# Maxima of self-attention carried for each half of the queries, and eight hidden units of the choice of tokens computed among its gates

## The chip, the cores and the metric

The kernel runs on one core of a Trainium2 chip, as one program. The metric is the time of a run on the device in microseconds (us); the median of three runs is given. A profiled execution gives the trace.

## The reference

Two decoder layers on x of 4 x 1024 tokens with 256 features. Each layer has self-attention, cross-attention and a feed-forward part with experts, each added to its input and followed by a layer norm. What the change touches:

```python
# layer 0, self-attention: 16 heads of 16 features, rotated q and k, causal
scores = jnp.einsum('bhqd,bhkd->bhqk', q, k) * scale
scores = jnp.where(causal, jnp.finfo(scores.dtype).min, scores)
out = jnp.einsum('bhqk,bhkd->bhqd', jax.nn.softmax(scores, axis=-1), v)

# layer 1, differential self-attention: 16 heads, two sets of q and k of 8 features, no mask
a = attend(q1, k1) - lam * attend(q2, k2)
a = a * rsqrt(mean(a * a) + eps) * rms_weight * (1.0 - LAMBDA_INIT)

# layer 1, expert choice: each expert takes 512 of the 1024 tokens of a batch
gate_scores = jax.nn.softmax(x @ w_gate_w + w_gate_b, axis=-1)
...
route = masked / denom * capacity
_, seq_ids = jax.lax.top_k(route_eb, K)
h = jax.nn.gelu(einsum('ebkd,edh->ebkh', xg, W1) + b1, approximate=False)
o = einsum('ebkh,ehd->ebkd', h, W2) + b2
```

## The kernel before

x stays in SBUF as X, 128 partitions by 32 tiles of tokens by 256 features. The stages run one after the other: self-attention (`attention`: `project`, `attend`, `merge`), cross-attention, experts, twice. In the second layer the experts are `expert_choice`: `choose` and `take`.

**`attend`.** It works on groups of four score rows s (four heads of a batch, or in the second layer two heads with two sets each): 16 groups in the first layer and 32 in the second. Queries come in two halves q of 512, keys in tiles of 128. A group has NS slots: 12 in the causal layer (four for q = 0, eight for q = 1, the diagonal ones with 512, 384, 256 and 128 columns) and 16 in the other. In a slot TensorE makes the four scores of one key tile and one half of the queries (line 739), in one of four banks psS each, and ScalarE turns each into exponentials (line 612); one or two slots later TensorE multiplies them by V (line 760), for which GpSimd cuts the diagonal blocks first (line 573). At the end of a half ScalarE copies the sum (line 633), TensorE turns it back (line 778), ScalarE copies that (line 628), VectorE inverts the sums (line 706) and GpSimd scales, squares and adds up.

The exponentials need the maximum of each query's scores. That is subtracted inside the score product: rows TOP and TOP + 1 of the operand Q hold the maxima in two parts, with rows of ones in K. So for each group the scores are also made with queries on the partitions (line 789, four products a slot, in two double banks psM), and VectorE reduces them, two reductions a slot (line 695, or line 689 where a block is masked), into `tops`. When all 2 x NS pairs of a group are done, `combine` (line 700) makes `negm`, 32 columns; TensorE turns it (line 798, 32 x 128), ScalarE copies it twice (line 620, rounded, and line 621), GpSimd subtracts one from the other (line 564), and the SyncE queue writes the rows into Q with eight DMAs (line 510).

What sets the order is written by hand: every engine walks the same turns. In turn t stand the maxima of group t in all slots, the scores of group t - 1 from slot LATE = 5 on, and those of group t - 2 before that. `turn_maxima`, `cut` and the rows of group t - 1 stand in slot 0 of turn t. Banks of psS go round in the order in which their contents are freed, and the list `taken` fixes it. The loads of the group after the next (lines 157 and 158, 16 DMAs) stand in the SyncE queue before the rows.

**`choose`.** X is turned in eight pieces (line 2565), ScalarE copies each to XT (line 2620), and TensorE makes the gates' logits (line 2574, 16 products of 8 columns a piece) for two halves h of the tiles. VectorE's chain makes routes of each half; ScalarE gives its exponentials (line 2625). Routes are turned (line 2592), and a search of 16 steps on VectorE, with a small product of TensorE in each (line 2610), finds the threshold of each expert; then VectorE makes the selection (line 2745). The hidden layer for all tokens is computed in 32 units (line 2585), with an activation Gelu on ScalarE each (line 2639): five units between the two turned routes, one in each step of the search, the rest after it. `take` starts with line 2785.

## Time and profile before

| | us |
|---|---|
| runs | 3478.0, 3486.63, 3487.77 |
| median | 3486.63 |
| the profiled execution, its time | 3496.01 |
| its span from the first instruction to the last | 3493.9 |
| first self-attention, `attend` | 132.9 to 624 |
| second self-attention, `attend` | 1275 to 2546 |
| `choose` | 3286.9 to 3401.5 |

Times in the trace are us from the start of the span. PE is TensorE, PEld its weight load, DVE VectorE, ACT ScalarE, POOL GpSimd, SPq the DMA queue of SyncE. A row of a timeline has the start, the duration with the tail of the last instruction, and the idle time before with what ended it; where instructions overlap, their durations do so too. The granted clock is 1.00 at 2.4 GHz and 0.50 at 1.2 GHz.

### The profile page before, as it was taken

To read this page: it belongs to the slowest core of one execution; us is meant where nothing else is said; L and a number is where in the kernel's file an instruction comes from. 1 tells how busy PE (TensorE), PEld (TensorE's weight loads), DVE (VectorE), ACT (ScalarE), POOL (GpSimd) and SP (SyncE) were. 2 spreads that over 40 slices of the span, in tenths; PEclk is the share of its full clock that TensorE was granted. 3 is DMA by queue.
4 is the path that set the end of the run, shared out by engine and by line. 5 is a ranking of instruction groups with operands and counts; after the bars stand their busy time and mean duration, and the time that the engine had idled before them with its cause. 6 is when DMAs were issued, how large, how long until landed. Compare 5 with 4: busy or idle time off the path is not lost. (4 is left out here: it accounts for less than half of the span.)

```text
span 3493.9 us, 63847 instructions
## 1 busy us (share of the span) xinstructions
PE 3160.6 (90%) x23976; PEld 1627.6 (47%) x23976; DVE 2756.2 (79%) x4703; ACT 2099.0 (60%) x4192; POOL 960.8 (27%) x1622
## 2 busy tenths in 40 slices
PE   7599999678499879999999999999968699999699
PEld 4244444444288533333333333333347454544546
DVE  7788886447677798999999999999557677776466
ACT  3178888245333226999999999999937233334130
POOL 4234433124333430111111111111132334445000
PEclk9699999878699977999999999999989899999789
DMA  4422220000000240010010010000003401000001
GB/s 167 137 53 65 65 59 21 28 1 1 25 1 1 94 140 20 21 29 20 21 30 20 20 29 21 20 26 24 2 20 121 149 26 51 26 26 1 17 1 48
DMA packets 69412, 143.97 MB, mean 41 GB/s; under 512 B 20752, under 2 KB 33872, under 8 KB 68976
## 3 DMA queue, kind: packets, MB, share of 16 engines
q1 hardware_dynamic: 64752, 135.70, 13.0%
q8 instruction: 189, 3.10, 0.4%
q10 hardware_dynamic: 4352, 4.20, 0.4%
q14 instruction: 119, 0.97, 0.1%
HBM read 83.07 MB, written 54.53 MB: 39 GB/s over the span
## 5 line engine op out<-in xcount | busy, mean ns | idle before, releaser
L612 ACT ACTIVATE L_parts<-L_attn_psS 128x512 f32<-128x512 f32 (+3 forms) x2816 | 1409.5, 573 | 146.5 <-PE L_attn_psS L739 104.2
L695 DVE TENSOR_REDUCE L_attn_tops<-L_attn_psM 128x2 f32<-128x1024 f32 x1152 | 1325.9, 1214 | 60.5 <-PE L_attn_psM L789 57.5
L789 PE MATMUL L_attn_psM<-L_K,L_Q 30*128 30x512 f32 (+4 forms) x2816 | 866.5, 492 | 63.7 <-PEq L199 27.2
L739 PE MATMUL L_attn_psS<-L_Q,L_K 32*128 32x512 f32 (+4 forms) x2816 | 876.3, 474 | 2.2 <-ACT L_parts L612 0.9
L760 PE MATMUL L_attn_psS<-L_parts,L_attn_V 128*32 128x256 f32 (+1 forms) x10752 | 855.6, 390 | 5.4 <-ACT L_parts L612 0.6
L739 PEld LDWEIGHTS L_attn_psS<-L_Q,L_K 32*128 32x128 f32 (+1 forms) x2816 | 408.4, 185 | 556.4 <-ACT L_parts L612 270.1
L789 PEld LDWEIGHTS L_attn_psM<-L_K,L_Q 30*128 30x128 f32 (+1 forms) x2816 | 389.2, 190 | 110.4 <-DVE L_attn_tops L695 58.7
L760 PEld LDWEIGHTS L_attn_psS<-L_parts,L_attn_V 128*32 128x32 f32 x10752 | 214.6, 108 | 354.6 <-issue 186.8
L689 DVE CUSTOM_DVE_ANT_0 L_attn_psM<-L_attn_psM,L_attn_wide 128x384 f32<-128x384 f32 (+3 forms) x512 | 236.5, 522 | 19.0 <-PE L_attn_psM L789 18.5
L2276 ACT ACTIVATE x_E<-x_psS 128x512 f32<-128x512 f32 x256 | 138.9, 595 | 184.3 <-PE x_psS L2399 170.7
L2322 DVE TENSOR_REDUCE x_tops<-x_psM 128x2 f32<-128x1024 f32 x128 | 153.2, 1206 | 92.5 <-PE x_psM L2428 92.4
L2238 POOL TENSOR_TENSOR x_acc<-x_acc,x_E 128x512 f32<-128x512 f32 x128 | 171.9, 1343 | 182.4 <-ACT x_E L2276 180.2
L1539 PE MATMUL m_psE<-m_wp,m_xp 128*128 128x512 f32 x768 | 182.1, 394 | 2.8 <-DVE m_z L1673 2.8
L573 POOL TENSOR_SCALAR_AFFINE_SELECT L_parts<-L_parts 128x128 f32<-128x128 f32 x512 | 146.4, 294 | 125.6 <-ACT L_parts L612 119.0
L564 POOL TENSOR_TENSOR L_attn_mparts<-L_attn_mT,L_attn_mparts 32x128 fp32r<-32x128 f32 x48 | 21.5, 449 | 567.3 <-ACT L_attn_mT L621 567.3
L544 POOL TENSOR_TENSOR L_attn_recs<-L_attn_rec,L_attn_sign 128x16 f32<-128x16 f32 x64 | 14.3, 223 | 575.1 <-DVE L_attn_rec L706 575.1
L2395 PE MATMUL x_psS<-x_Q,x_K 64*128 64x512 f32 x864 | 150.5, 438 | 11.4 <-ACT x_E L2276 11.4
L1539 PEld LDWEIGHTS m_psE<-m_wp,m_xp 128*128 128x128 f32 x768 | 142.6, 189 | 34.6 <-DVE m_z L1673 5.7
L2448 PE MATMUL x_psO<-x_E,L1x_VL 128*64 128x512 f32 x512 | 145.3, 647 | 0.0
L2395 PEld LDWEIGHTS x_psS<-x_Q,x_K 64*128 64x128 f32 x864 | 75.0, 190 | 144.8 <-ACT x_E L2276 94.5
L2428 PE MATMUL x_psM<-x_K,x_Q 64*128 64x512 f32 x768 | 118.2, 406 | 23.3 <-DMA x_K<-L1x_kTc 20.4
L324 PE MATMUL L_proj_psQ<-L_AO,L_proj_wqk 128*128 128x512 f32 x256 | 125.0, 614 | 15.4 <-DMA L_AO<-in_L_sin 12.2
(363 smaller groups left out, 4131.7 us busy)
## 6 DMA issues: line engine op xcount, KB each, us to landing
parts_q<-L_parts SPq DMA_DIRECT2D x64, 256.0 KB
parts_k<-L_parts SPq DMA_DIRECT2D x64, 256.0 KB
L_Q<-parts_q SPq DMA_DIRECT2D x192, 64.0 KB
L_K<-parts_k SPq DMA_DIRECT2D x192, 64.0 KB
L_Q<-parts_q SPq DMA_DIRECT2D x64, 128.0 KB
L_K<-parts_k SPq DMA_DIRECT2D x64, 128.0 KB
queries<-x1p_qo SPq DMA_DIRECT2D x16, 512.0 KB, 3.5
keys<-x1p_ko SPq DMA_DIRECT2D x16, 512.0 KB, 4.4
```

Source lines behind the costliest of these rows:

```text
L573: pool.affine_select(block, block, [[1, P]], ALU.is_ge, 0.0, base=0, channel_multiplier=-1).then_inc(e_cut, 1)
L612: act.activation(E[(4 * n + s) % (4 * RING)][:, c0:], psS[bank][:, c0:], ACT.Exp, scale=scale).then_inc(e_done, 1)
L689: last = dve.tensor_tensor_reduce(part, part, wide[:, HALF - n:], 1.0, LOWEST, ALU.add, ALU.max, tops[:, row, h:h + 1])
L695: dve.tensor_reduce(dst, src, AX, ALU.max).then_inc(m_read, 1)
L739: pe.matmul(psS[bank][:, c0:], K[g.slot][r:r + RH, c, kt * P:(kt + 1) * P], Q[g.slot][r:r + RH, c, q * HALF + c0:(q + 1) * HALF], start=Tr ...
L760: last = pe.matmul(psS[bank_of["O", at, q]][32 * s:32 * s + 32, lo:hi], V[g.slot][:, kt, s // shared, :], E[(4 * n + s) % (4 * RING)][:, l ...
L789: last = pe.matmul(psM[bank][:, j * HALF:j * HALF + n], Q[t.slot][r:r + TOP, c, qt * P:(qt + 1) * P], K[t.slot][r:r + TOP, c, h * HALF:h * ...
L1539: last = pe.matmul(psE[e][:], xp[u.slot][:, i, c, k * P:(k + 1) * P], wp[:, j, c, e * HALF:(e + 1) * HALF], start=(n + c == 0), stop=(n == ...
L2238: pool.tensor_tensor(to[:], to[:], e[:], ALU.add).then_inc(sums[1], 1)
L2322: dve.tensor_reduce(dst[:, :, t, h], src, AX, ALU.max).then_inc(m_read, 1)
L2395: pe.matmul(banks[h][:], K[k][rows, x, kt * P:(kt + 1) * P], Q[k][rows, y, cols], start=(j == 0), stop=False, skip_group_check=True)
L2448: last = pe.matmul(psO[LD * h:LD * h + LD, :], v, tile(s, h)[:], start=(kt == 0), stop=(kt == TB), skip_group_check=True)
```

## The change

In `attend` the pairs of the maxima are put in order of the halves: all those of q = 0 first. Each half has its own combine (line 703 after the change, a maximum of two halves of `tops`, 16 columns, no negation; the blank rows of K become -1 in place of 1), its own transpose of 16 x 128, one copy by ScalarE, a rounding copy and a subtraction on GpSimd, and its own row DMAs: four in the first layer and two in the second. The combine stands between the two reductions of a slot: slots 4 and 12 after the group's first in the first layer, 8 and 16 in the second. The scores of a group begin LAG = 12 slots after its first maxima, in both layers (17 and 21 before); those of its second half four and eight slots later. The turns give way to one loop over slots. The loads of the next group but one stand between the rows of a group's second half and those of the next one's first.

In `choose` eight of the 32 hidden units stand in the loop of the gates, one after each piece, in the two halves of psR; their activations stand between the copies of XT and around the exponentials.

```diff
-                    pool.memset(K[k][:].bitcast(F32), 1.0).then_inc(blank, 1)
+                    pool.memset(K[k][:].bitcast(F32), -1.0).then_inc(blank, 1)
...
+    of_half = [sum(t // 4 == q for _, t, _, _, _ in pairs) for q in range(2)]
...
-    LATE = 5
+    LATE = 4
+    LAG = max(of_half[0] // 2 + LATE, NS + LATE - (ends[0] + 1))
...
+        B_AT = [LAG + BACK + ends[0] + 3 - BACK, LAG + BACK + ends[1] + 2]
+        SLOTS = groups * NS + B_AT[1] - NS + 4
...
+        T_AT = [of_half[0] // 2, NS]
+        SUM_AT = LAG + BACK
...
+                def cut(g, q):
+                    pt, done = mparts[q][g % 2], 2 * (2 * g + q)
+                    pool.wait_ge(e_done, freed["T", g, q])
...
+                    pool.tensor_copy(pt[:, 0, :], mT[q][g % 2][:]).then_inc(m_cut, 1)
+                    pool.wait_ge(m_cut, done + 1)
+                    pool.tensor_tensor(pt[:, 1, :], mT[q][g % 2][:], pt[:, 0, :].bitcast(F32), ALU.subtract).then_inc(m_cut, 1)
...
-                    act.activation(mparts[k][:, 0, :], psS[bank][0:4 * TB, 0:P], ACT.Copy).then_inc(m_cut, 1)
-                    act.activation(mT[k][:], psS[bank][0:4 * TB, 0:P], ACT.Copy).then_inc(e_done, 1)
+                    act.activation(mT[q][g % 2][:], psS[bank][0:16, 0:P], ACT.Copy).then_inc(e_done, 1)
...
-                    dve.tensor_reduce(negm[t.slot][:], tops[:], AX, ALU.max, negate=True).then_inc(m_neg, 1)
+                    dve.tensor_tensor(most_of[q][g % 2][:], tops[:, q, :, :, 0], tops[:, q, :, :, 1], ALU.max).then_inc(m_most, 1)
...
-                    pe.transpose(psS[bank][0:4 * TB, 0:P], negm[g % 3][:], ident[:]).then_inc(s_done, 1)
+                    pe.transpose(psS[bank][0:16, 0:P], most_of[q][g % 2][:].rearrange("p s t -> p (s t)"), ident[:]).then_inc(s_done, 1)
...
+        EARLY = NB
+        hidden_bank = lambda n: psR[:, n % 2 * HALF:(n % 2 + 1) * HALF] if n < EARLY else psH[n % 4]
...
                     gates(n)
+                    hidden(n)
                 turned_routes(0)
-                todo = iter(range(UNITS))
+                todo = iter(range(EARLY, UNITS))
...
-                for n in range(6):
-                    copied(n)
-                exponents(0)
-                for n in range(6, NB):
-                    copied(n)
+                copied(0)
+                for n in range(EARLY):
+                    if n + 1 < NB:
+                        copied(n + 1)
+                    if n == 4:
+                        exponents(0)
+                    rectified(n)
                 exponents(1)
```

On VectorE in the second self-attention, the kernel before: reductions of maxima, the combine of a group and the two inversions.

```order
L695 TENSOR_REDUCE L_attn_tops<-L_attn_psM 128x2 x16
L706 RECIPROCAL L_attn_rec<-L_attn_ob 128x16
L695 TENSOR_REDUCE L_attn_tops<-L_attn_psM 128x2 x12
L700 TENSOR_REDUCE L_attn_negm<-L_attn_tops 128x32
L695 TENSOR_REDUCE L_attn_tops<-L_attn_psM 128x2 x4
L706 RECIPROCAL L_attn_rec<-L_attn_ob 128x16
L695 TENSOR_REDUCE L_attn_tops<-L_attn_psM 128x2 x16
```

The same place after the change:

```order
L703 TENSOR_TENSOR L_attn_most<-L_attn_tops 128x16
L690 TENSOR_REDUCE L_attn_tops<-L_attn_psM 128x2
L696 RECIPROCAL L_attn_rec<-L_attn_ob 128x16
L690 TENSOR_REDUCE L_attn_tops<-L_attn_psM 128x2 x15
L703 TENSOR_TENSOR L_attn_most<-L_attn_tops 128x16
L690 TENSOR_REDUCE L_attn_tops<-L_attn_psM 128x2
L696 RECIPROCAL L_attn_rec<-L_attn_ob 128x16
```

The one combine of a group has become two of half the width, each one reduction ahead of the end of its slot.

On TensorE at the transpose of the maxima in the second self-attention, before (psS holds scores and sums, psM the maxima's products):

```order
L739 MATMUL L_attn_psS<-L_Q,L_K 128x512
L789 MATMUL L_attn_psM<-L_K,L_Q 128x512
L760 MATMUL L_attn_psS<-L_parts,L_attn_V 32x256 x4
L798 MATMUL L_attn_psS<-ident,L_attn_negm 32x128
L739 MATMUL L_attn_psS<-L_Q,L_K 128x512
L789 MATMUL L_attn_psM<-L_K,L_Q 128x512
```

And after:

```order
L732 MATMUL L_attn_psS<-L_Q,L_K 128x512
L774 MATMUL L_attn_psM<-L_K,L_Q 128x512
L752 MATMUL L_attn_psS<-L_parts,L_attn_V 32x256 x4
L783 MATMUL L_attn_psS<-ident,L_attn_most 16x128
L732 MATMUL L_attn_psS<-L_Q,L_K 128x512
L774 MATMUL L_attn_psM<-L_K,L_Q 128x512
```

The transpose stands at the end of a slot as before, with 16 rows in place of 32, and comes twice a group in place of once (every 82 rows in place of 163).

On TensorE in the gates loop of `choose`, before, its last rounds and what follows (each unit of the hidden layer is two products here):

```order
L2565 MATMUL f_psT<-ident,X 128x128 x8
L2574 MATMUL f_psG<-f_wg,f_XT 128x8 x8
L2565 MATMUL f_psT<-ident,X 128x128 x8
L2574 MATMUL f_psG<-f_wg,f_XT 128x8 x16
L2592 MATMUL f_psR<-ident,f_routes 128x128 x4
L2585 MATMUL f_psT<-f_XT,f_w 128x512 x10
L2592 MATMUL f_psR<-ident,f_routes 128x128 x4
```

And after:

```order
L2559 MATMUL f_psG<-f_wg,f_XT 128x8 x8
L2572 MATMUL f_psR<-f_XT,f_w 128x512 x2
L2550 MATMUL f_psT<-ident,X 128x128 x8
L2559 MATMUL f_psG<-f_wg,f_XT 128x8 x8
L2572 MATMUL f_psR<-f_XT,f_w 128x512 x2
L2559 MATMUL f_psG<-f_wg,f_XT 128x8 x8
L2572 MATMUL f_psR<-f_XT,f_w 128x512 x2
L2580 MATMUL f_psR<-ident,f_routes 128x128 x4
L2572 MATMUL f_psT<-f_XT,f_w 128x512 x10
L2580 MATMUL f_psR<-ident,f_routes 128x128 x4
```

Each round has got a hidden unit, in psR; the five units between the turned routes have stayed, and the tail after the search has eight products in place of 24.

On ScalarE in the same loop, before:

```order
L2620 ACTIVATE f_XT<-f_psT 128x2x512 x6
L2625 ACT_TABLE_LOAD
L2625 ACTIVATE f_ex<-f_less 128x4x32
L2620 ACTIVATE f_XT<-f_psT 128x2x512 x2
L2625 ACTIVATE f_ex<-f_less 128x4x32
L2635 ACTIVATE L1f_B<-f_b 32x1024
L2636 ACTIVATE f_b2h<-f_b 32x1024
L2639 ACT_TABLE_LOAD
L2639 ACTIVATE L1f_HT<-f_psT,f_b 128x512 x32
```

And after, from the fourth activation on:

```order
L2616 ACTIVATE L1f_HT<-f_psR,f_b 128x512
L2609 ACTIVATE f_XT<-f_psT 128x2x512
L2621 ACT_TABLE_LOAD
L2621 ACTIVATE f_ex<-f_less 128x4x32
L2616 ACT_TABLE_LOAD
L2616 ACTIVATE L1f_HT<-f_psR,f_b 128x512
L2609 ACTIVATE f_XT<-f_psT 128x2x512
L2616 ACTIVATE L1f_HT<-f_psR,f_b 128x512
L2609 ACTIVATE f_XT<-f_psT 128x2x512
L2616 ACTIVATE L1f_HT<-f_psR,f_b 128x512 x2
L2621 ACT_TABLE_LOAD
L2621 ACTIVATE f_ex<-f_less 128x4x32
```

The two exponentials stand amid the activations now, with a table load on either side of each.

## Rows read from the trace of the kernel before

**Rows 1.** The page, busy time, share of the span and instructions of each engine
```profile
PE 3160.6 (90%) x23976; PEld 1627.6 (47%) x23976; DVE 2756.2 (79%) x4703; ACT 2099.0 (60%) x4192; POOL 960.8 (27%) x1622
```

**Rows 2.** The page, costliest groups: busy, mean ns of one, idle before, releaser
```profile
L612 ACT ACTIVATE L_parts<-L_attn_psS 128x512 f32<-128x512 f32 (+3 forms) x2816 | 1409.5, 573 | 146.5 <-PE L_attn_psS L739 104.2
L695 DVE TENSOR_REDUCE L_attn_tops<-L_attn_psM 128x2 f32<-128x1024 f32 x1152 | 1325.9, 1214 | 60.5 <-PE L_attn_psM L789 57.5
```

**Rows 3.** Windows: busy us of PE, PEld, DVE, ACT, POOL; granted clock; DMA; GB/s
```profile
1275.00:1360.00 85.00, 69.15 (x325) 22.76 (x325) 73.98 (x70) 25.37 (x47) 3.20 (x10) 0.50 0.10 29
1500.00:1800.00 300.00, 298.76 (x3126) 119.17 (x3127) 294.54 (x278) 284.48 (x558) 49.31 (x144) 1.00 0.09 23
3290.00:3330.00 40.00, 34.82 (x167) 34.82 (x167) 8.45 (x69) 8.77 (x9) 0.00 (x0) 0.50 0.10 29
1036.00:1045.00 9.00, 9.00 (x53) 7.68 (x52) 7.61 (x20) 2.96 (x5) 2.97 (x3) 1.00 0.01 4
```

**Rows 4.** Timeline, VectorE, second self-attention: start, us, instruction, idle before it
```profile
1330.66 1.23 DVE L695 TENSOR_REDUCE L_attn_tops<-L_attn_psM 128x2 f32<-128x1024 f32 x1 [0.51 <-PE L_attn_psM L789]
...
1815.13 0.22 DVE L700 TENSOR_REDUCE L_attn_negm<-L_attn_tops 128x32 f32<-128x64 f32 x1
...
1818.06 2.36 DVE L695 TENSOR_REDUCE L_attn_tops<-L_attn_psM 128x2 f32<-128x1024 f32 x2 [0.24 <-PE L_attn_psM L789]
...
2494.23 0.22 DVE L700 TENSOR_REDUCE L_attn_negm<-L_attn_tops 128x32 f32<-128x64 f32 x1
```

**Rows 5.** Timeline, ScalarE, second self-attention
```profile
1817.34 0.27 ACT L620 ACTIVATE L_attn_mparts<-L_attn_psS 32x128 fp32r<-32x128 f32 x1
1817.52 0.25 ACT L621 ACTIVATE L_attn_mT<-L_attn_psS 32x128 f32<-32x128 f32 x1
...
1819.02 2.09 ACT L612 ACTIVATE L_parts<-L_attn_psS 128x512 f32<-128x512 f32 x4 [0.17 <-PE L_attn_psS L739]
...
1855.07 0.27 ACT L620 ACTIVATE L_attn_mparts<-L_attn_psS 32x128 fp32r<-32x128 f32 x1
...
2545.64 0.60 ACT L628 ACTIVATE L_attn_ob<-L_attn_psS 128x512 f32<-128x512 f32 x1 [0.75 <-PE L_attn_psS L778]
```

**Rows 6.** Timeline, ScalarE, first self-attention
```profile
198.15 0.25 ACT L621 ACTIVATE L_attn_mT<-L_attn_psS 32x128 f32<-32x128 f32 x1
...
225.92 0.25 ACT L621 ACTIVATE L_attn_mT<-L_attn_psS 32x128 f32<-32x128 f32 x1
...
229.63 1.66 ACT L612 ACTIVATE L_parts<-L_attn_psS 128x384 f32<-128x384 f32 x4 [0.30 <-PE L_attn_psS L739]
...
234.80 1.57 ACT L612 ACTIVATE L_parts<-L_attn_psS 128x512 f32<-128x512 f32 x3 [0.72 <-PE L_attn_psS L739]
...
622.57 0.60 ACT L628 ACTIVATE L_attn_ob<-L_attn_psS 128x512 f32<-128x512 f32 x1 [0.75 <-PE L_attn_psS L778]
```

**Rows 7.** Timeline, SyncE's queue and VectorE, first self-attention
```profile
226.72 6.22 SPq L510 DMA_DIRECT2D L_Q<-L_attn_mparts  x8
...
584.55 0.22 DVE L700 TENSOR_REDUCE L_attn_negm<-L_attn_tops 128x32 f32<-128x64 f32 x1
```

**Rows 8.** Timeline, TensorE, choice of tokens
```profile
3295.18 1.97 PE L2565 MATMUL f_psT<-ident,X 128*128 128x128 f32 x8 [6.34 <-DMA L1f_w<-in_L1f_w]
...
3333.71 1.09 PE L2592 MATMUL f_psR<-ident,f_routes 128*128 128x128 f32 x4
...
3379.58 20.85 PE L2585 MATMUL f_psT<-f_XT,f_w 128*128 128x512 f32 x48
3401.46 0.70 PE L2785 MATMUL f1t_psS<-L1f_sel,L1f_onehot 32*128 32x512 f32 x2 [1.03 <-PEq L2538]
```

**Rows 9.** Timeline, ScalarE and VectorE, choice of tokens
```profile
3318.29 1.28 ACT L2625 ACT_TABLE_LOAD   x1
...
3400.47 0.69 ACT L2639 ACTIVATE L1f_HT<-f_psT,f_b 128x512 f32<-128x512 f32 x1 [1.03 <-PE f_psT L2585]
...
3385.84 1.23 DVE L2745 TENSOR_TENSOR L1f_sel<-f_tie,f_gt 128x1024 fp32r<-128x1024 bf16 x1
```

More of the change, by code:

```diff
@@ L429, in attend @@
-        lam_sign = sems.sem(f"{tag}_attn_lam_sign")
-        def run(turn):
-            for g in range(groups + 2):
-                turn(At(g, None, 3), g < groups, 1 <= g <= groups, g >= 2)
+        sem = lambda name: sems.sem(f"{tag}_attn_{name}")
+        v_blank, t_blank = sem("v_blank"), sem("t_blank")
+        maskin, masks = sem("maskin"), sem("masks")
+        mx = [[sem(f"mx{q}{k}") for k in range(2)] for q in range(2)]
+        v_in = sem("v_in")
+        s_done = sem("s_done")
+        e_done, e_cut = sem("e_done"), sem("e_cut")
@@ new lines, in attend, with at @@
+        passed = sem("passed")
+        o_done = sem("o_done")
+        o_rec, o_sign, o_scaled, o_norm = sem("o_rec"), sem("o_sign"), sem("o_scaled"), sem("o_norm")
+        m_done, m_read = sem("m_done"), sem("m_read")
+        m_most, m_cut = sem("m_most"), sem("m_cut")
+        lam, lamin, lam_sign = sem("lam"), sem("lamin"), sem("lam_sign")
+        B_AT = [LAG + BACK + ends[0] + 3 - BACK, LAG + BACK + ends[1] + 2]
+        SLOTS = groups * NS + B_AT[1] - NS + 4
+        def at(slot, offset, length=NS):
+            g, k = divmod(slot - offset, NS)
+            return (g, k) if 0 <= g < groups and k < length else None
@@ L436, in cuts, with event, group @@
+        def event(slot, offset):
+            return slot >= offset and (slot - offset) % NS == 0 and (slot - offset) // NS < groups
+        def group(slot, offset):
+            return (slot - offset) // NS
+        T_AT = [of_half[0] // 2, NS]
+        SUM_AT = LAG + BACK
         def cuts(g, n):
-            return g.times(4 * sum(diagonal), 4 * sum(diagonal[:n]))
-        def in_turn(new, last):
-            return range(NS if new or last else LATE + BACK + 4)
+            return g * 4 * sum(diagonal) + 4 * sum(diagonal[:n])
@@ new lines, in attend @@
+        for slot in range(SLOTS):
+            exp, summed = at(slot, LAG), at(slot, SUM_AT)
+            if exp:
+                left += [exp + (s,) for s in range(4)]
+                taken += [exp + (s,) for s in range(2)]
+            if summed and (summed[1] == 0 or summed[1] - 1 in ends):
+                taken.append(("O", summed[0], steps[summed[1]][0]))
+            if exp:
+                taken += [exp + (s,) for s in range(2, 4)]
+            for q in range(2):
+                if event(slot, T_AT[q]):
+                    taken.append(("T", group(slot, T_AT[q]), q))
+                    left.append(("T", group(slot, T_AT[q]), q))
+            if summed and summed[1] in ends:
+                left.append(("O", summed[0], steps[summed[1]][0]))
+            for q in (1, 0):
+                if event(slot, B_AT[q]):
+                    taken.append(("B", group(slot, B_AT[q]), q))
+                    left.append(("B", group(slot, B_AT[q]), q))
@@ L513, in _, with rows @@
-                run(turn)
-                for k in range(3):
-                    n = len(range(k, groups, 3))
-                    sp.wait_ge(mx[k], 128 * n)
+                def rows(g, q):
+                    sp.wait_ge(m_cut, 2 * (2 * g + q) + 2)
+                    for j in range(2):
+                        for c in range(NQ):
+                            to = Q[g % 3][TOP + j:TOP + j + (HP - 1) * RH + 1:RH, c, q * HALF:(q + 1) * HALF]
+                            src = mparts[q][g % 2][c * 4 * HP:(c + 1) * 4 * HP, j, :]
+                            sp.dma_start(to.bitcast(F32), src.bitcast(F32)).then_inc(mx[q][g % 2], 16)
@@ new lines, in _ @@
+                load_group(sp, keep, dh, 1)
+                for g in range(groups):
+                    if g >= 1:
+                        rows(g - 1, 1)
+                        if g + 1 < groups:
+                            if g == 2:
+                                for k in range(4):
+                                    sp.wait_ge(parts_out[k], 256)
+                            if g >= 2:
+                                sp.wait_ge(s_done, s_at[g - 2, NS - 1, 3] + 1)
+                            load_group(sp, keep, dh, g + 1)
+                    rows(g, 0)
@@ L518, in _ @@
+                rows(groups - 1, 1)
+                for q in range(2):
+                    for k in range(2):
+                        sp.wait_ge(mx[q][k], ROWS * (groups // 2))
             @block.gpsimd
@@ L764, in product @@
                         last.then_inc(o_done, 1)
-                def products(t, n, last, old, half):
-                    j = n - LATE - BACK
-                    if j >= 0 and last:
-                        product(t.base - 1, j, half)
-                    if j < 0 and old:
-                        product(t.base - 2, NS + j, half)
                 def turn_back(g, q):
```

319 lines of the change are left out of this document (126 added, 193 removed).

## The prediction

> **What bounds the kernel now.** I read the page's shares first: TensorE is busy for 90% of the span, VectorE for 79%, ScalarE for 60% [rows 1]. Averages hide the stages, so next come the costliest groups: the exponentials of self-attention (2816 of 0.573 us) and the reductions of its maxima (1152 of 1.214 us, and the reader sees there that 57.5 of their 60.5 us of idle time end with a maxima product of TensorE) [rows 2]. Then the windows. In the steady part of the second self-attention (16 slots a group, 32 groups) 300 us hold 298.76 us of TensorE, 294.54 of VectorE and 284.48 of ScalarE [rows 3]: three engines full at once, so a microsecond taken from one of them alone is worth little, and what counts there is how many slots there are and what fills them. From the copy of one group's maxima to the next takes 1855.07 - 1817.34 = 37.73 us, 2.357 a slot [rows 5]; two reductions take 2.36 with their tail, 2.27 from start to start [rows 4]. The filling stands at a clock of 0.50 (1275 to 1360), where mixed reductions of 1.23 us follow 1.74 us apart, each after 0.51 us for TensorE, that is 3.48 us a slot against 2.357 [rows 3, 4]. Last comes the choice of tokens. There the token searches end with the selection at 3385.84 + 1.23 = 3387.07, but TensorE has 48 hidden products (12 units of four) left at 3379.58, for 20.85 us, and the taking of tokens starts at 3401.46 [rows 8, 9]: TensorE's tail is what is late, by 14.4 us.
>
> **Part 1, a shorter lag in the second layer.** A group's scores may start when its maxima lie in Q's rows. Before, that was 21 slots after its first maximum (16 + 5); by halves it is 12 (8 + 4). So nine slots of maxima alone leave the start and nine of scores alone leave the end, and nine slots in which both run come in. Maxima alone cost the reductions, 2.27. Scores alone: from the last combine at 2494.23 to the last copy back at 2545.64 are 51.4 us for some 22 slots, 2.33 each [rows 4, 5]. 9 x (2.27 + 2.33 - 2.357) = 20.2 us less. Nothing hides these; they are the path itself.
>
> **Part 2, the steady group of the second layer.** VectorE's one combine (0.22) becomes two of half the output, which read 32 values and not 64 a partition; not shown, so between 0.09 each (the smallest step beside it) and 0.22; I take 0.15, no change. ScalarE's two copies (0.27 and 0.25, 0.43 from start to end, and soon after them 0.17 us of waiting for TensorE's late scores) become one copy at each of two places: between 2 x 0.20 and 2 x 0.50 against 0.75 now [rows 5]. TensorE gets a second transpose of some 0.2 us. GpSimd gets a second subtraction and two rounding copies; it is busy for 27% of the span and has time [rows 1]. The new wait is TensorE's: the transpose stands at the end of the slot between whose two reductions the combine was made. Queued behind it are the next slot's scores, and ScalarE waits for these. Before, the combine was 2.0 us old at that place (1815.13 + 0.22 to the copy at 1817.34); now it is only one reduction old, so the transpose may wait up to 0.3. Behind a transpose VectorE had 0.24 us of idle time [rows 4]. Per group -0.35 to +0.25 us, -11 to +8 over 32; between like ends I take zero.
>
> **Part 3, the first layer.** The lag goes from 17 slots to 12. A group takes 226.17 - 198.40 = 27.8 us here (the copies' ends), 2.31 a slot; the end of the stage, from the last combine at 584.55 to 622.57, has 38 us in some 17 slots, 2.2 each, and the start, all reductions, I take at 1.95, since the half-masked ones are short. 5 x (1.95 + 2.2 - 2.31) = 9 us less [rows 6, 7]. Against it stands the wait for the rows. The second half's transpose comes at the end of slot 0, its scores at slot 4: three slots of narrow scores (384, 256 and 128 columns), and those before 234.80, of the same widths, ran from 229.63: 5.2 us, which VectorE's masked reductions may make 6.3. What must fit: the copy, 0.25; GpSimd's two steps, 0.8 (from the copy's end at 226.17 to SP's first row at 226.72, with the one of now between, are 0.55); four row DMAs of 6.22 / 8 = 0.78 each, 3.1; and their landing. Before, the eight were issued until 226.72 + 6.22 = 232.94 and the scores' exponential came at 234.80, so landing is at most 1.9 [rows 6, 7]. Sum 6.1: from nothing to 0.9 us late per group. VectorE's slots of the first half are now all masked ones, at their densest just there, and the second transpose finds ScalarE without work in store (its 0.72 us of idle time at 234.80 says so). I take 0.8 us a group between 0.3 and 1.1, x16 = +13. SP's queue: the 16 loads of the next group stand between the two halves' rows, 12 us at the price of a row, and the first half's rows are due eight slots after their transpose (18 us), so that they hide; if that cover went, each microsecond would be paid 15 times. The first layer gives -9 + 13 = +4 (-4 to +9).
>
> **Part 4, eight hidden units earlier in the choice.** The tail shrinks from 12 units to 4: 8 x 20.85 / 12 = 13.9 us less, and selection and TensorE then end together, 3387 against 3386.5, so the cover is gone exactly: a ninth unit would have brought nothing. The eight units are paid in the gates loop. It ran from 3295.18 to 3333.71, 38.5 us, all of it at a clock of 0.50 though TensorE was 87% busy [rows 3, 8], 5.0 us a round. At full clock, twice as fast, a round is 2.5 plus a unit of 1.74, 4.25 us; eight of these less the first transposes, 0.9, make 33.1. At half clock all along it is 38.5 + 8 x 3.44 = 66. The trace doesn't show which; the nearest row is the experts' stretch 1036 to 1045, where dense products, transposes and gate products alternate at 1.00 [rows 3]. I take one round at half clock: 37.4, or -1.1. On ScalarE the exponentials now stand amid the hidden units' activations, and the table is loaded twice more, 1.28 us each [rows 9]. The first pair is hidden under the loop. The second half's exponential stands behind the last early unit and its activation: 1.74 + 0.69 + 1.28, less some 0.9 that VectorE's subtraction of the maxima needs in that time anyway, +2.8, and VectorE's chain, the search and the selection shift by it. Net -13.9 - 1.1 + 2.8 = -12.2, from -16 to +16.
>
> The Trainium skill speaks against this part. "TensorE: Matmul & The Clock Gate", Part 4, says that a transpose on TensorE doesn't count as busy as other products do, and Part 1 that the gate's default is the throttled one, released by activity. By that rule a loop of which much is transposes keeps the low clock; the 0.50 under 87% agrees with it, the 1.00 at 1036 does so only if the dense products between hold the clock up. By the rule at its strictest this part would give +16 and not -12.2.
>
> **Sum.** -20.2 + 0 + 4 - 12.2 = -28.4 us: 3496.0 to 3467.6 for the profiled execution. That one stood 9.4 above the median of the runs, so 3486.6 - 28.4 = 3458 for a median. GpSimd's squares, which the change's name speaks of, are not in the diff; they bring nothing.
>
> **Rivals.** (a) The gates loop stays at half clock throughout. For it: the 38 us at 0.50. Against: 1036 to 1045. Then part 4 is +27.5 + 2.8 - 13.9 = +16 and the whole -20.2 + 4 + 16 = 0: 3487. (b) Each half's transpose, and its rows, stall TensorE. The mechanism: a transpose that waits for a combine only one reduction old, behind it the scores, behind these ScalarE with at most four banks in store; twice a group, 96 times in all. I priced it at zero and 0.8. If it is 0.6 us a transpose in both layers, 48 x 1.2 = 58 us stand against -20.2 - 9 - 12.2 = -41: +17, 3503. It decides from 41 / 48 = 0.86 us a group. For it: VectorE has only 0.7 us of room in a group of 37.7. Against: scores were hardly waited for before, and at slot 1 ScalarE's idle time was 0.17. (c) The low clock at the start of the second self-attention, 33 us at 3.48 a slot, cost about 11 us; the mixed work starts nine slots earlier and the clock may rise sooner or later after it: 10 us either way, 3448 or 3468. (d) The lag isn't shorter because something else holds the first scores, the loads say: then part 1 is gone, 3478. The loads of the second group are issued before, which speaks against it; I count it to (a).
>
> **How the numbers follow.** 0.3% is 10.5 us, about what a measurement of this kernel can tell from no change. The forecast 0.50; (c) 0.16, faster too; (a) with (d) 0.18, within 0.3%; (b) 0.16, slower. So 0.66, 0.18, 0.16. The low end is the forecast with the best of parts 2 and 4 and of (c): about 3435. The high end takes in (a) whole, 3487, and half of (b)'s way up, 3496; beyond it and below the low end lie 2 in 10. The likeliest case's own range is 3445 to 3472.
>
> **What would show it.** Part 1: in the second self-attention the first exponential 9 slots, some 20 us, earlier after the first reduction, and 12 to 13 slots from the last combine to the last copy. Part 2: a steady group of 37.4 to 38.0 us; 38.9 or more is (b), and the idle time would stand before the transposes as a wait for VectorE. Part 3: 28.2 to 28.9 us a group in the first layer, with a wait for the row DMAs at slot 4. Part 4: a granted clock near 1.00 from the second round of the gates loop, four units after the last search, and the taking of tokens 10 to 16 us earlier after the weights' landing; 0.50 in that loop is (a). The forecast is wrong if a steady group moves by more than 0.5 us, since that alone is 16 us.

## The result, and the profile after

The changed kernel takes 3465.2 us in the median of ten runs (3454.1 to 3474.0); the kernel before, run beside it, 3488.3 (3478.0 to 3495.7). The ratio is 0.9926 with a 95% interval of 0.9912 to 0.9941: 0.74% faster, 23 us by the medians, 26 by the ratio. The forecast was 3458, 28 us less, in a range of 3435 to 3496. The profiled execution has a span of 3459.2 us against 3493.9, 34.7 less: the one of before ran 7.7 us over the median 3488.3, the one of after 4.3 under its own. By stages of the two traces:

| stage | before | after | difference | forecast |
|---|---|---|---|---|
| first self-attention, `attend` | 490.7 | 486.9 | -3.8 | +4 |
| second self-attention, `attend` | 1271.4 | 1258.2 | -13.2 | -20.2 |
| end of the merge to the start of `take` | 121.8 | 108.1 | -13.7 | -12.2 |
| `take` to the end | 92.4 | 89.7 | -2.7 | 0 |
| everything else | 1517.6 | 1516.3 | -1.3 | 0 |

The last two rows are not touched by the diff. `take` has a stretch at the low clock at its start, whose length differs from run to run (its time was 88.1 to 92.4 us in the traces of this study), and the stages between vary by some us too.

The page of the changed kernel, with its shares and the two groups of [rows 1, 2] (columns: busy, mean ns of one, idle before):

```profile
PE 3128.2 (90%) x24024; PEld 1605.3 (46%) x24024; DVE 2762.1 (80%) x4751; ACT 2103.1 (61%) x4195; POOL 1004.0 (29%) x1766
...
L613 ACT ACTIVATE L_parts<-L_attn_psS 128x512 f32<-128x512 f32 (+3 forms) x2816 | 1410.4, 573 | 159.2 <-PE L_attn_psS L732 100.8
L690 DVE TENSOR_REDUCE L_attn_tops<-L_attn_psM 128x2 f32<-128x1024 f32 x1152 | 1343.3, 1218 | 74.6 <-PE L_attn_psM L774 68.3
```

The shares hardly moved; exponentials and reductions cost what they cost. The windows of [rows 3] again, and two more at the start of the second self-attention (columns: length, busy us of PE, PEld, DVE, ACT, POOL, granted clock):

```profile
1275.00:1360.00 85.00, 77.78 (x604) 28.79 (x604) 79.21 (x80) 53.83 (x104) 8.89 (x26) 0.75 0.09 22
1300.00:1316.00 16.00, 16.00 (x108) 4.71 (x109) 11.73 (x12) 10.14 (x20) 0.43 (x2) 0.50 0.00 1
1316.00:1320.00 4.00, 4.00 (x44) 1.32 (x36) 3.54 (x4) 3.25 (x7) 0.30 (x1) 0.83 0.24 56
1500.00:1800.00 300.00, 298.76 (x3104) 119.54 (x3096) 293.47 (x284) 280.41 (x551) 56.73 (x168) 1.00 0.09 23
3290.00:3330.00 40.00, 36.29 (x192) 24.17 (x192) 19.70 (x144) 20.79 (x25) 2.34 (x1) 1.00 0.00 1
```

The same place of the kernel before, behind the window that [rows 3] shows:

```profile
1360.00:1365.00 5.00, 5.00 (x45) 2.25 (x41) 3.70 (x4) 3.92 (x9) 0.00 (x0) 0.81 0.00 0
```

The reader is to see three things. ScalarE has 53.8 us of work between 1275 and 1360 in place of 25.4: the scores start earlier. The clock rises between 1316 and 1320, where before it rose between 1360 and 1365: the mixed work (maxima and scores together, from the first exponential on) begins at 1298.7 and runs for 19 us at 1.2 GHz; before, it began at 1324.1 and ran so for 38. The prediction's 33 us were too few: its window ended at 1360, ahead of the rise. And 3290 to 3330, all at 0.50 before, is at 1.00 now.

ScalarE's timeline around the transpose of a half's maxima, and the same half's a group later (the counterpart of [rows 5]):

```profile
1828.40 2.86 ACT L613 ACTIVATE L_parts<-L_attn_psS 128x512 f32<-128x512 f32 x5
1831.15 0.25 ACT L620 ACTIVATE L_attn_mT<-L_attn_psS 16x128 f32<-16x128 f32 x1
...
1869.32 0.25 ACT L620 ACTIVATE L_attn_mT<-L_attn_psS 16x128 f32<-16x128 f32 x1
```

A group takes 1869.32 - 1831.15 = 38.17 us, where it was 37.73. Once the clock is up, that is constant to some 0.02 us over the stage. For 31 groups it makes +13.6 us, two thirds of what the shorter lag gives. VectorE's combine beside it (as [rows 4]):

```profile
1830.45 0.17 DVE L703 TENSOR_TENSOR L_attn_most<-L_attn_tops 128x16 f32<-128x16 f32 x1
1830.54 1.22 DVE L690 TENSOR_REDUCE L_attn_tops<-L_attn_psM 128x2 f32<-128x1024 f32 x1
```

The combine costs VectorE 0.09 us. TensorE there, with the products and scores of each half slot (maxima's products left out):

```profile
1830.21 0.64 PE L752 MATMUL L_attn_psS<-L_parts,L_attn_V 128*32 128x256 f32 x8
1830.78 0.28 PE L783 MATMUL L_attn_psS<-ident,L_attn_most 128*16 128x128 f32 x1
1830.99 0.50 PE L732 MATMUL L_attn_psS<-L_Q,L_K 32*128 32x512 f32 x1
...
1831.32 0.50 PE L732 MATMUL L_attn_psS<-L_Q,L_K 32*128 32x512 f32 x1
...
1831.74 0.64 PE L752 MATMUL L_attn_psS<-L_parts,L_attn_V 128*32 128x256 f32 x8
...
1832.74 0.64 PE L752 MATMUL L_attn_psS<-L_parts,L_attn_V 128*32 128x256 f32 x8
```

Without a transpose the groups of eight products follow 1.00 us apart (1831.74 to 1832.74) or 1.24; across the transpose 1830.21 to 1831.74 are 1.53. Two things make that up. The transpose itself holds TensorE from 1830.78 to the first score at 1830.99, 0.21 us. And the second score starts 0.33 us behind the first: the transpose has taken one of the four banks psS, and the bank of this score comes free only when ScalarE's exponential ends, at 1828.40 + 2.86 = 1831.26. Between 1400 and 2480 all 56 transposes of the maxima are followed by such a pair, 0.31 us apart in the median, and each time the trace names an exponential as what released the second score. It isn't the only place: in the half slots of 1.00 us the two scores start together, in those of 1.2 and 1.3 they are 0.18 and 0.25 us apart too.

The first self-attention (ScalarE's copies of two successive groups and the first exponentials of the second half's wide slots, then SyncE's rows; the counterparts of [rows 6, 7]):

```profile
198.64 0.27 ACT L620 ACTIVATE L_attn_mT<-L_attn_psS 16x128 f32<-16x128 f32 x1 [0.18 <-PE L_attn_psS L783]
...
226.74 0.27 ACT L620 ACTIVATE L_attn_mT<-L_attn_psS 16x128 f32<-16x128 f32 x1 [0.18 <-PE L_attn_psS L783]
...
233.75 2.06 ACT L613 ACTIVATE L_parts<-L_attn_psS 128x512 f32<-128x512 f32 x4
```

```profile
227.91 2.11 SPq L501 DMA_DIRECT2D L_Q<-L_attn_mparts  x4
```

A group takes 28.10 us where it took 27.8. The four rows are issued from 227.91 to 230.02, the scores that need them stand some 3.5 us later, and the waits of this stretch hold none for a row DMA.

The choice of tokens (TensorE; as [rows 8]), then ScalarE's exponentials of the second half and VectorE's selection (as [rows 9]):

```profile
3277.21 1.97 PE L2550 MATMUL f_psT<-ident,X 128*128 128x128 f32 x8 [6.29 <-DMA L1f_w<-in_L1f_w]
...
3285.80 1.55 PE L2550 MATMUL f_psT<-ident,X 128*128 128x128 f32 x8
...
3290.69 1.04 PE L2550 MATMUL f_psT<-ident,X 128*128 128x128 f32 x8
...
3361.40 7.11 PE L2572 MATMUL f_psT<-f_XT,f_w 128*128 128x512 f32 x16
3369.55 1.15 PE L2781 MATMUL f1t_psS<-L1f_sel,L1f_onehot 32*128 32x512 f32 x4 [1.03 <-PEq L2523]
```

```profile
3318.29 0.31 ACT L2621 ACTIVATE f_ex<-f_less 128x128 f32<-128x128 f32 x1
...
3367.66 1.22 DVE L2741 TENSOR_TENSOR L1f_sel<-f_tie,f_gt 128x1024 fp32r<-128x1024 bf16 x1
```

The clock rises within the transposes at 3285.80 (1.55 us, then 1.04 in each later round), and from 3290.69 on a round takes 4.38 us. After the last search four units are left, 7.11 us; the selection ends at 3368.9 and `take` starts at 3369.55.

VectorE's copies of the turned routes, before and after:

```profile
3345.64 0.69 DVE L2712 COPY f_v<-f_psR 128x512 f32<-128x512 f32 x1 [1.67 <-PE f_psR L2592]
```

```profile
3326.71 1.46 DVE L2708 COPY f_v<-f_psR 128x512 f32<-128x512 f32 x2
```

Before, VectorE waited 1.67 us for TensorE's second turned routes; now it doesn't wait there.

### The profile page after: what moved, and what is told of

Same layout as the page of the kernel before. It is cut to its first block and busy times, and to the rows that moved or that the text cites. A ratio compares the mean times of both kernels' runs of the same rounds, so it can differ in the third digit from the quotient of the medians.

```text
span 3459.2 us, 64315 instructions
## 1 busy us (share of the span) xinstructions
PE 3128.2 (90%) x24024; PEld 1605.3 (46%) x24024; DVE 2762.1 (80%) x4751; ACT 2103.1 (61%) x4195; POOL 1004.0 (29%) x1766
## 3 DMA queue, kind: packets, MB, share of 16 engines
q1 hardware_dynamic: 62448, 135.69, 13.2%
## 5 line engine op out<-in xcount | busy, mean ns | idle before, releaser
L690 DVE TENSOR_REDUCE L_attn_tops<-L_attn_psM 128x2 f32<-128x1024 f32 x1152 | 1343.3, 1218 | 74.6 <-PE L_attn_psM L774 68.3
L774 PEld LDWEIGHTS L_attn_psM<-L_K,L_Q 30*128 30x128 f32 (+1 forms) x2816 | 402.6, 187 | 86.6 <-DVE L_attn_tops L684 29.5
L542 POOL CAST L_attn_mparts<-L_attn_mT 16x128 fp32r<-16x128 f32 x96 | 27.0, 281 | 1032.6 <-ACT L_attn_mT L620 1031.8
L684 DVE CUSTOM_DVE_ANT_0 L_attn_psM<-L_attn_psM,L_attn_wide 128x128 f32<-128x128 f32 (+3 forms) x512 | 237.6, 517 | 13.9 <-PE L_attn_psM L774 13.0
L1522 PEld LDWEIGHTS m_psE<-m_wp,m_xp 128*128 128x128 f32 x768 | 142.6, 189 | 34.7 <-DVE m_z L1656 5.8
L324 PE MATMUL L_proj_psQ<-L_AO,L_proj_wqk 128*128 128x512 f32 x256 | 125.9, 618 | 15.1 <-DMA L_AO<-in_L_sin 13.2
L2411 PE MATMUL x_psM<-x_K,x_Q 64*128 64x512 f32 x768 | 118.0, 406 | 23.5 <-DMA x_K<-L1x_kTc 20.5
L230 POOL TENSOR_TENSOR L_proj_rot<-L_AO 128x512 f32<-128x512 f32 x64 | 109.5, 1711 | 94.1 <-DVE L_AO L284 94.1
```

What stands on the lines that cost most here:

```text
L684: last = dve.tensor_tensor_reduce(part, part, wide[:, HALF - n:], 1.0, LOWEST, ALU.add, ALU.max, tops[:, q, s + j, t, h:h + 1])
L690: dve.tensor_reduce(dst, src, AX, ALU.max).then_inc(m_read, 1)
L774: last = pe.matmul(psM[bank][:, j * HALF:j * HALF + n], Q[g % 3][r:r + TOP, c, qt * P:(qt + 1) * P], K[g % 3][r:r + TOP, c, h * HALF:h * H ...
L1522: last = pe.matmul(psE[e][:], xp[u.slot][:, i, c, k * P:(k + 1) * P], wp[:, j, c, e * HALF:(e + 1) * HALF], start=(n + c == 0), stop=(n == ...
```

## The experiments

All are compared with the kernel before on their own chip. Each stage time is from one profiled execution. Those of the second self-attention differ by some us for a reason that the edits don't set out to change: in the twelve traces with the new attention the clock rises 6 to 22 us after the first exponential, in the two with the old one (before and e1) 38 us after it. The time of a steady group is free of that, so the readings below go by it.

### The parts alone

The choice of tokens of the changed kernel in the kernel before (e1), and the self-attentions of the changed kernel with the choice of before (e2).

> Only the choice of tokens is changed (eight hidden units among its gates); both self-attentions are those of before. Theory A (the parts are independent): choose is 14 us shorter, the rest the same, some 14 us under before, ratio 0.996. Theory B (a good part of the 14 us came from the clock's state that the shorter attention left behind): under 8 us, and a granted clock of 0.50 in later rounds of the gates loop.

> Only the two self-attentions are changed; the choice of tokens is that of before. Theory A: 4 us less in the first layer's, 13 in the second's, some 12 to 17 us under before, ratio 0.996, with a gates loop of 38.5 us at a clock of 0.50 as before. Theory B: the gates loop comes out faster than 38.5 us here too, and less than 12 us are left for choose_only.

Measured: e1 3472.8 us, ratio 0.9949 (0.9929 to 0.9969); from the merge's end to `take` 106.6 us against 121.8. e2 3480.0, ratio 0.9961 (0.9942 to 0.9981); `choose` 122.5 with the gates at the low clock, the self-attentions 488.4 and 1259.0. The product of the ratios is 0.991, near 0.9926. The parts add up within the intervals, theory A: e1's gates loop is at full clock with the old attention, and e2's at the low one with the new.

### The first layer as it was

`attend_whole` is the `attend` of the kernel before.

```diff
-            attend(nc, a, keep, sems, f"L{layer}", dh, groups, layer == 0)
+            (attend_whole if layer == 0 else attend)(nc, a, keep, sems, f"L{layer}", dh, groups, layer == 0)
```

> The changed kernel with the first layer's self-attention as it was (one combine, one transpose and eight row DMAs a group, lag 17). If the first layer brought 4 us (9 from the lag less 5 from 0.32 us a group), this one is 4 us over the changed kernel, its groups take 27.8 us and not 28.1, and the second layer is untouched at 38.17 us a group. If the first layer's change is worth nothing or costs, as I forecast (+4), it is equal or up to 4 us faster than the changed kernel.

Measured: 3461.5 us, ratio 0.9916 (0.9886 to 0.9945). By the times of the runs it can't be told from the changed kernel. In the traces the first layer takes 491.5 us with groups of 27.79, against 486.9 with the changed one. Over all traces of this study, from the first maxima product to the last inversion, the ten with the changed layer have 482.5 to 491.2 us, 488 on average, and the three with the old one 490.6, 491.3 and 496.9, 493 on average: some 5 us of gain, with ranges that touch. My +4 is not borne out; that it is a gain rests on the traces alone.

### What makes a group of the second layer 0.44 us longer

First theories: the transpose waits for a combine only one reduction old (W), or ScalarE's second event costs (S). The control has one slot more of lag (e5), and in e6 the transpose and all behind it move one slot away from the combine.

```diff
-    LATE = 4
+    LATE = 4 if causal else 5
...
+        TURN_AT = T_AT if causal else [t + 1 for t in T_AT]
...
-                        if event(slot, T_AT[q]):
-                            turn_maxima(group(slot, T_AT[q]), q)
+                        if event(slot, TURN_AT[q]):
+                            turn_maxima(group(slot, TURN_AT[q]), q)
```

> The changed kernel with one slot more between a half's transpose and its scores in the second layer (LATE = 5, lag 13); the control for e6. Both theories: a group stays at 38.17 us, one slot more of lag, 2.2 us more in the second self-attention.

> As e5, and the transpose, ScalarE's copy and GpSimd's part stand one slot after the combine, which stays. Theory W (the 0.44 us a group more in the second layer are the transpose's wait for a combine only one reduction old): the wait is gone, a group takes 37.8 to 37.9 us, 10 us less over the stage than e5. Theory S (they are ScalarE's and TensorE's second event itself, a copy of 0.25 with 0.12 us of idle time before it and 0.23 behind it): a group stays at 38.1 to 38.2.

Measured: e5 3466.6 us, ratio 0.9931 (0.9907 to 0.9955), 38.17 us a group; e6 3460.7, ratio 0.9930 (0.9906 to 0.9955). ScalarE's copies of e6, one group apart:

```profile
1821.84 0.25 ACT L621 ACTIVATE L_attn_mT<-L_attn_psS 16x128 f32<-16x128 f32 x1
...
1860.00 0.25 ACT L621 ACTIVATE L_attn_mT<-L_attn_psS 16x128 f32<-16x128 f32 x1
```

38.16 us. W has fallen: with the combine a whole slot old, the group is no shorter. Then a second copy on ScalarE:

```diff
+                    if not causal:
+                        act.activation(spare[q][:], psS[bank][0:16, 0:P], ACT.Copy).then_inc(spared, 1)
                     act.activation(mT[q][g % 2][:], psS[bank][0:16, 0:P], ACT.Copy).then_inc(e_done, 1)
```

> The changed kernel with a second, unused copy of each transpose by ScalarE in the second layer (0.18 us from start to start, twice a group). Theory S: ScalarE's time is paid in full, a group takes 38.17 + 0.36 = 38.5 us, 11 us more over the stage. Theory W: ScalarE has 2 us of idle time a group and hides the copies, 38.2.

Measured: 3464.8 us, ratio 0.9939 (0.9914 to 0.9964). The two copies of a half, and the first of them a group later:

```profile
1816.93 0.25 ACT L625 ACTIVATE L_attn_spare<-L_attn_psS 16x128 f32<-16x128 f32 x1
1817.09 0.25 ACT L626 ACTIVATE L_attn_mT<-L_attn_psS 16x128 f32<-16x128 f32 x1
...
1855.09 0.25 ACT L625 ACTIVATE L_attn_spare<-L_attn_psS 16x128 f32<-16x128 f32 x1
```

38.16 us again. S has fallen for ScalarE's part: 0.16 us more on it, twice a group, add nothing; it waits for TensorE there anyway. What is left is the transpose, and e9 takes it away in the second layer after the first group, so that the later groups' exponentials have the first group's maxima:

```diff
+        TURNED = groups if causal else 1
...
-                        if event(slot, T_AT[q]):
+                        if event(slot, T_AT[q]) and group(slot, T_AT[q]) < TURNED:
                             turn_maxima(group(slot, T_AT[q]), q)
```

> The changed kernel; in the second layer the transposes of the maxima on TensorE and ScalarE's copies of them are left out after the first group (GpSimd waits for the combine and splits the first group's maxima again, so the later groups' exponentials have the wrong maxima). The second copy on ScalarE cost nothing and the later transpose neither. Theory P (what a group pays for is TensorE's transpose, 0.44 us each with the half slot that follows it): a group takes 38.17 - 0.88 = 37.3 us, 27 us less over the stage, unless VectorE's 32 reductions (36.3) with inversions and combines (0.8) hold it at 37.1. Theory Q (the new order of the pairs or the loop over slots costs it, not the transposes): a group stays at 38.2 or loses less than 0.3.

Measured: 3436.1 us, ratio 0.9856 (0.9824 to 0.9889), the stage 1232.1 us. ScalarE's copies back, one group apart:

```profile
1822.31 0.60 ACT L632 ACTIVATE L_attn_ob<-L_attn_psS 128x512 f32<-128x512 f32 x1 [0.21 <-PE L_attn_psS L768]
...
1859.63 0.60 ACT L632 ACTIVATE L_attn_ob<-L_attn_psS 128x512 f32<-128x512 f32 x1 [0.22 <-PE L_attn_psS L768]
```

1859.63 - 1822.31 = 37.32 us, over the stage 37.31 in the median: theory P to 0.02 us. One event costs (38.17 - 37.31) / 2 = 0.43 us, and the kernel before, with one, stands at 37.73 = 37.31 + 0.42. That is the whole difference; the order of the pairs and the loop over slots cost nothing, and neither do GpSimd's second split and the second row DMAs, which e9 keeps. e9 leaves ScalarE's copy out as well; a second one was free in e8. And it leaves out the transpose's turn in the four banks. So 0.43 us is the price of TensorE's 0.21 and of the wait for a bank behind it together; no run takes one away and leaves the other.

### Where the transposes stand

In e7 they move, with lag 12, to the middle of the next slot.

```diff
+        TURN_AT = T_AT if causal else [t + 1 for t in T_AT]
+        MID = not causal
...
+                        for q in range(2):
+                            if s == (1 if MID else 3) and event(slot, TURN_AT[q]):
+                                turn_maxima(group(slot, TURN_AT[q]), q)
```

> The changed kernel (lag 12 in the second layer), but the transpose, ScalarE's copy and GpSimd's part stand in the middle of the slot after the combine's, between the second and the third score, so that the first half of the products is not between. Theory S with the idle time around the copy as its larger part: that idle time, 0.35 a transpose, shrinks or not with the place; if it goes, a group takes 37.5 to 37.8 us, 12 to 20 us less over the stage; if the event costs the same anywhere, 38.17. Theory W: 37.8 to 37.9. The rows have 2.5 slots, 5.9 us, instead of 3.

Measured: 3481.0 us, ratio 0.9973 (0.9956 to 0.9991), 38.69 us a group, slower than all I had named. GpSimd there, and TensorE's largest wait of a kind that the others don't have (us in total, times, longest):

```profile
1815.66 0.22 POOL L562 TENSOR_TENSOR L_attn_recs<-L_attn_rec,L_attn_sign 128x16 f32<-128x16 f32 x1 [15.36 <-DVE L_attn_rec L708]
...
1818.84 0.28 POOL L549 CAST L_attn_mparts<-L_attn_mT 16x128 fp32r<-16x128 f32 x1
...
PEld L_attn_psS L744 <- DMA L_Q<-L_attn_mparts: 41.4, 46, 1.2
```

ScalarE's copy was ready at 1816.2, but GpSimd stood in the scaling, the squares and the sums of a finished half, six steps from 1815.66 on, and split the maxima only at 1818.84; the rows came late and the scores waited for them. So the run doesn't answer its question. It shows something else: in the changed kernel the split stands just ahead of that row of steps in GpSimd's order, and one slot later it stands behind it.

In e10 the transposes back, four in a row at the end of a half, come two slots later, directly behind those of the maxima.

```diff
         B_AT = [LAG + BACK + ends[0] + 3 - BACK, LAG + BACK + ends[1] + 2]
+        if not causal:
+            B_AT = [b + 2 for b in B_AT]
```

> The changed kernel; in the second layer the transposes back stand two slots later, in the same slots as those of the maxima, right behind them. If the slow half slot behind a transpose (scores 0.33 us apart instead of together) is paid once for both, a group takes 37.7 us, 14 us less over the stage; if each transpose costs its own time wherever it stands, 38.17; if ScalarE with two more copies in one slot becomes late, 38.5 or more.

Measured: 3443.9 us, ratio 0.9889 (0.9863 to 0.9914), the stage 1235.0. TensorE at the joint place, and ScalarE's copies a group apart:

```profile
1809.18 0.64 PE L754 MATMUL L_attn_psS<-L_parts,L_attn_V 128*32 128x256 f32 x8
1809.79 0.28 PE L785 MATMUL L_attn_psS<-ident,L_attn_most 128*16 128x128 f32 x1
1810.02 0.63 PE L765 MATMUL L_attn_psS<-ident,L_attn_oT 128*128 128x128 f32 x4
1810.58 0.50 PE L734 MATMUL L_attn_psS<-L_Q,L_K 32*128 32x512 f32 x1
...
1810.58 0.50 PE L734 MATMUL L_attn_psS<-L_Q,L_K 32*128 32x512 f32 x1
...
1829.00 0.25 ACT L622 ACTIVATE L_attn_mT<-L_attn_psS 16x128 f32<-16x128 f32 x1
...
1866.54 0.25 ACT L622 ACTIVATE L_attn_mT<-L_attn_psS 16x128 f32<-16x128 f32 x1
```

37.54 us a group, 0.64 less, beyond the 0.44 that I had named. From the products at 1809.18 to the next at 1811.01 are 1.83 us for both kinds. In the changed kernel they take 1.53 and 1.59 apart from each other (the second is 1844.29 to 1845.88 there), where a half slot without a transpose takes 1.14 on average: 0.69 in place of 0.84 a half. The two scores behind the joint place start together again, both at 1810.58, and the trace names no exponential that the second waited for. The other 0.17 a half isn't seen at the place itself; the half slots without a transpose are each 0.01 us shorter (1.13), and what makes them so isn't shown. Of the stage's 23 us, 20 are the groups and 3 the clock, which rose 8 us after the first exponential and not 19.

e12 does the same in both layers (`B_AT = [24, 28]` in the first).

> The changed kernel with the transposes back in the same slots as those of the maxima, right behind them, in both layers (six and one slots later in the first layer). In the second layer as in e10, 37.53 us a group. In the first, if the break in TensorE's order is paid once for both there too, a group takes 27.4 to 27.8 us and not 28.10, 5 to 10 us less over the stage, some 3436 in all; if in the first layer the rows and the wide slots of ScalarE set the time, 28.1 stays and the whole is as e10, 3444.

Measured: 3438.1 us, ratio 0.9859 (0.9840 to 0.9878), the fastest complete kernel here, 51 us under the kernel before. The first layer's groups take 28.00 us and not 28.10: there it is worth 0.1 and not 0.3 to 0.7, and its stage 485.1 us. Nearly all of it is the second layer.

### The choice of tokens

e11 has four early units in place of eight.

```diff
-        EARLY = NB
+        EARLY = NB // 2
...
                     gates(n)
-                    hidden(n)
+                    if n < EARLY:
+                        hidden(n)
```

> The changed kernel with four of the hidden units in the gates loop instead of eight, in its first four rounds. If four more units stand in the tail, the taking starts 4 x 1.74 = 7 us later after the search, and the loop is 4 x 1.74 = 7 us shorter: choose as a whole 0 to +2 us if the clock stays at 1.00 in the last four rounds without a unit. If the hidden units are what holds the clock up, it falls back to 0.50 in these rounds, each then 5.0 us and not 2.6, and choose is some 5 to 9 us longer than the changed kernel's 108.

Measured: 3468.8 us, ratio 0.9951 (0.9934 to 0.9967), `choose` 113.0 us against 108.1. TensorE's gate products in the sixth round, and the windows:

```profile
3307.24 2.47 PE L2559 MATMUL f_psG<-f_wg,f_XT 128*128 128x8 f32 x16
...
3300.00:3305.00 5.00, 5.00 (x37) 4.00 (x35) 0.87 (x3) 2.15 (x4) 0.00 (x0) 1.00 0.00 0
3305.00:3310.00 5.00, 5.00 (x40) 5.00 (x40) 2.36 (x24) 3.43 (x4) 0.00 (x0) 0.83 0.00 0
3310.00:3315.00 5.00, 5.00 (x27) 5.00 (x25) 4.66 (x43) 1.02 (x1) 0.00 (x0) 0.50 0.01 3
```

The last early unit ends at 3303.9. The fifth round, without a unit, still has the granted clock of 1.00; in the sixth it falls (its gate products take 2.47 us, those of the last two rounds 3.42 each), and the rest of the loop runs at 1.2 GHz with TensorE busy throughout. So the units hold the clock up: in this loop e11 and the changed kernel differ in nothing else that TensorE does.

e4 puts the second half's exponentials ahead of the last early activation.

```diff
+                    if n == EARLY - 1:
+                        exponents(1)
                     rectified(n)
-                exponents(1)
```

> The changed kernel with the second half's exponentials ahead of the last early unit's activation. If the exponential's place behind that activation is what makes VectorE's chain late (1.74 + 0.69 + table load of 1.28), the second half's exponentials come 2 to 3 us earlier after the end of the gates, and search, selection and the start of the taking shift by as much: 2 to 3 us under the changed kernel. If TensorE's units bound that stretch, the exponentials come earlier and the taking starts at the same time.

Measured: 3468.0 us, ratio 0.9932 (0.9905 to 0.9959), `choose` 108.0 against 108.1. ScalarE, VectorE and GpSimd:

```profile
3321.49 0.31 ACT L2621 ACTIVATE f_ex<-f_less 128x128 f32<-128x128 f32 x1 [0.67 <-DVE f_less L2657]
...
3326.30 1.98 DVE L2676 CAST f_ixf<-f_ix 128x32 f32<-128x32 uint32 x1
...
3333.63 0.69 DVE L2709 COPY f_v<-f_psR 128x512 f32<-128x512 f32 x1 [1.24 <-PE f_psR L2580]
...
3325.89 2.35 POOL L2541 TENSOR_TENSOR L1f_B<-f_b,f_b2h 32x1024 fp32r<-32x1024 f32 x1 [47.96 <-ACT f_b2h L2635]
```

The exponentials do start 2.8 us earlier: 3321.49 is 1.0 after VectorE began on the gates (3320.52), where it was 3318.29 - 3314.47 = 3.8. Then the gain is lost twice. VectorE's cast takes 1.98 us in place of 0.18 and ends at 3328.28, 0.04 us after GpSimd's subtraction of 2.35 beside it, which it had missed before; and the second copy of the routes waits 1.24 us for TensorE, which has five units ahead of it. That the cast waited for the subtraction is read from these two ends alone; no run takes one of them away. The Trainium skill ("SBUF — State Buffer", section "SBUF: two separate sides") says that VectorE and GpSimd share a pair of ports that one of them holds for a whole instruction; these rows agree with it, as far as two ends 0.04 us apart can.

## Why the prediction was right, point by point

**What bounds the kernel.** Right in naming three full engines in the second self-attention and wrong in not asking which of them a microsecond is taken from. e8 and e9 answer it for this step: 0.16 us more on ScalarE twice a group are free, a transpose on TensorE is paid in full and with it the wait for a bank, 0.43.

**Part 1.** The lag was sized well. The first exponential comes 28.1 us after the stage's start and not 48.6: -20.5 for filling, against 9 slots of 2.27. From the last combine to the last copy are 30 us and not 51.4. Against these stand the nine more slots in which both run, as forecast.

**Part 2.** This step failed in its size and in its reason. I took zero between -11 and +8; it was +13.6. The bounds themselves were wrong: -0.35 to +0.25 a group is ScalarE's copies alone ("between 2 x 0.20 and 2 x 0.50 against 0.75 now"), and TensorE's second transpose ("of some 0.2 us") stands in no term of the sum, nor does the bank it takes. The event costs 0.43 us of the group, also where the transpose stands a slot behind the combine, and rival (b), which I tied to the wait for the combine, had the price in view (0.6 each) and the mechanism wrong in that; its scores that come late behind the transpose are in the trace.

**Part 3.** The rows are not late; a group costs +0.31 us and not +0.8, so -4 and not +4. What failed is the sum of 6.1 us: a row DMA was issued in 0.53 us and not in 0.78, and landing was taken at its upper bound. The 0.31 may be the same transpose, which e12 recovers only a third of; that is open.

**Part 4.** Right in its main terms: one round of the gates loop at half clock, then 1.00; four units after the search; selection and TensorE's tail ending together. VectorE gets the last gates 37.3 us after the loop's start and not 38.7, -1.5 where I had -1.1, and ScalarE's exponentials are late by what I said, 3.8 - 1.0 us. But I let that lateness reach the selection, and it doesn't: the selection ends 91.7 us after the loop's start, before it was 91.9. The kernel before lost as much at its second turned routes, 1.67 us of waiting for TensorE, and that wait is gone. e4 shows the same from the other side: with the exponentials early, VectorE waits there for 1.24 us. Measured -13.7, forecast -12.2. One reading was loose: the loop of before was not 87% busy but fully, since the window of [rows 3] begins 5 us ahead of it.

**The Trainium skill's rule** ("TensorE: Matmul & The Clock Gate", Part 4, on transposes) agrees with e11, for a mix of transposes and gate products: with these alone the clock fell to 0.50 at a fully busy TensorE. It didn't decide the sum, because with a unit in every round this loop stayed at 1.00.

**Rival (c)** came too: the clock rose after 19 us of mixed work and not 38. A slot takes some 3.3 us there in place of 2.36, so that this gave some 6 us and hides nearly half of part 2's error; why the clock rises sooner isn't shown. The total is closer than its parts by luck: the second layer gave 7 us less than forecast and the first 8 us more.

## What to carry to other kernels

Where three engines are each over 93% busy, what an added step costs is found by adding or taking away work on one at a time: doubling ScalarE's copy cost nothing, and leaving TensorE's transposes out gave back the whole difference. Count the bank that a step takes as well as its time. Small transposes between streams of products are worth putting side by side; here it gave more (0.64 us a group, 20 us in all) than the restructuring of the maxima in that stage. Before moving a step by one slot, look at what stands ahead of it on every engine it passes, GpSimd too.

## What was unexpected of the hardware

A 16 x 128 transpose, 0.28 us long by its row, costs 0.43 us of a group between matmuls of scores and products, and the second score behind it waits for a bank each time. Busy time alone doesn't tell TensorE's clock: the gates loop with a hidden unit in each round ran at 2.4 GHz from its third round on, and without units it ran at 1.2 GHz in the kernel before and fell to that in e11's last rounds, TensorE fully busy in all of them. And the mixed work of the second self-attention, TensorE busy throughout, stood at 1.2 GHz for 38 us before and for 6 to 22 us in the traces with the new attention.
